# A four-layer hybrid kernel on one core: the first state-space steps are put in another order, and two of them move inside the branches of the feed-forward phase before

## The reference

```python
x = x + _L0_attn_a_ref(_layernorm(x), ...)   # a gated delta rule, in 256 steps of a recurrence
x = x + _L0_ffn_ref(_layernorm(x), ...)      # silu(x @ Wg.T) * (x @ Wu.T) @ Wd.T, hidden size 384
x = x + _L0_attn_b_ref(_layernorm(x), ...)   # a state-space layer (below)
x = x + _L0_ffn_ref(_layernorm(x), ...)      # the same feed-forward weights again
```

```python
zxbcdt = hidden_states @ W_in
z, xBC, dt = ...                                   # 256, 512 and 4 columns
xBC = jax.nn.silu(_causal_dwconv(xBC, conv_w, conv_b))   # 4 taps along the tokens
dt = jax.nn.softplus(dt + dt_bias)                 # the steps, one for each of 4 heads
A = -jnp.exp(A_log)
y = _ssd(x, dt, A, Bm, Cm) + x * D[None, None, :, None]  # sums over the past, decaying by exp(sums of dt * A)
y = y * jax.nn.silu(z)
y = y * jax.lax.rsqrt(jnp.mean(y * y, axis=-1, keepdims=True) + EPS) * norm_w
return y @ W_out
```

## Time and profile before

| | us |
|---|---|
| median of 3 runs | 880.91 (879.55 to 883.13) |
| the profiled execution | 879.69 |
| its span, first to last instruction | 877.9 |
| so around the span | 1.8 |
| PE busy | 773.3 (88%) |
| DVE busy | 621.8 (71%) |
| ACT busy | 535.7 (61%) |
| POOL busy | 561.6 (64%) |

### The profile page before, as it was taken

One profiled execution on the slowest core, in us unless ns is written; L12 is line 12 of the kernel. 1 busy time (PEld: TensorE's weight loads), 2 busy tenths in 40 slices (PEclk: granted clock), 3 DMA queues, 4 the chain that ended last, 5 costly groups with the idle time before them and its releaser, 6 DMA issues. The chain is left out here.

```text
span 877.9 us, 16088 instructions
## 1 busy us (share of the span) xinstructions
PE 773.3 (88%) x5146; PEld 551.7 (63%) x5146; DVE 621.8 (71%) x1739; ACT 535.7 (61%) x1035; POOL 561.6 (64%) x901
## 2 busy tenths in 40 slices
PE   1369999999999895999856999999999999959997
PEld 1258888888888774666634456656555555545665
DVE  1357878777878753888664678888887777637885
ACT  2224443443345323888644878978887788828986
POOL 1267567666766620788711579778868876757785
PEclk9979999999999999999955899999999999979999
DMA  7511111111111100000000000000000000000112
GB/s 195 134 28 37 46 28 28 38 46 28 28 42 41 29 14 1 1 1 0 2 0 8 1 1 3 7 1 2 9 0 1 7 4 1 1 0 25 48 49 73
DMA packets 59420, 22.16 MB, mean 25 GB/s; under 512 B 22224, under 2 KB 59088, under 8 KB 59344
## 3 DMA queue, kind: packets, MB, share of 16 engines
q1 hardware_dynamic: 59344, 21.23, 9.5%
HBM read 11.59 MB, written 9.63 MB: 24 GB/s over the span
## 5 line engine op out<-in xcount | busy, mean ns | idle before, releaser
L1405 DVE SCALAR_TENSOR_TENSOR arena<-bank,convw_sb,arena 128x510 f32<-128x510 f32 (+2 forms) x192 | 142.4, 744 | 42.2 <-ACT arena L898 37.5
L667 POOL TENSOR_TENSOR arena<-arena 128x768 f32<-128x768 f32 x64 | 114.9, 1815 | 12.8 <-ACT arena L925 10.9
L641 POOL TENSOR_TENSOR arena<-ff,arena 128x512 f16<-128x512 f32 x64 | 73.6, 1159 | 23.0 <-ACT arena L867 21.0
L571 POOL TENSOR_TENSOR leaf_tmp<-leafV 32x14 f32<-32x14 f32 (+6 forms) x224 | 55.8, 249 | 37.1 <-DMA leafV<-LT_dram 21.8
L862 ACT ACTIVATE ff<-bank 128x512 f32<-128x512 f32 x96 | 56.2, 586 | 32.2 <-PE bank L1708 32.0
L770 ACT ACTIVATE ff<-bank 128x256 f32<-128x256 f32 (+2 forms) x80 | 33.9, 424 | 65.1 <-PE bank L1549 37.7
L575 POOL TENSOR_TENSOR leafV<-leafV,leaf_tmp 32x14 f32<-32x14 f32 (+6 forms) x224 | 62.3, 278 | 17.6
L1795 PE MATMUL bank<-xnT,win_sb 128*128 128x512 f32 x128 | 71.8, 645 | 0.0
L1221 DVE SCALAR_TENSOR_TENSOR ff<-bank,ff 128x512 f32<-128x512 f32 x96 | 64.6, 684 | 8.9 <-ACT ff L862 8.0
L919 ACT ACTIVATE arena<-bank 128x384 f32<-128x384 f32 x128 | 59.8, 492 | 15.5 <-PE bank L1810 15.3
L755 ACT ACTIVATE xnT<-bank 128x512 f32<-128x512 f32 x34 | 20.3, 596 | 79.1 <-PE bank L1536 79.0
(11 more groups left out here) (199 smaller groups left out, 2239.2 us busy)
## 6 DMA issues: line engine op xcount, KB each, us to landing
LT_dram<-arena SPq DMA_DIRECT2D x16, 256.0 KB, 2.4
ff<-R_dram SPq DMA_DIRECT2D x16, 256.0 KB, 3.0
out<-x_all SPq DMA_DIRECT2D x8, 512.0 KB, 3.2
x_all<-in_L_attn_a_x SPq DMA_DIRECT2D x7, 512.0 KB, 7.3
ff<-pieces_dram SPq DMA_DIRECT2D x48, 6.0 KB
x_all<-in_L_attn_a_x SPq DMA_DIRECT2D x2, 256.0 KB, 3.6
R_dram<-tab SPq DMA_DIRECT2D x2, 256.0 KB, 2.7
leafV<-LT_dram SPq DMA_DIRECT2D x16, 32.0 KB, 2.7
```

What stands on the lines that cost most here:

```text
L571: nc.gpsimd.tensor_tensor(prod, V[:, s:s + 1, s + 1:LEAF].broadcast_to([leaf_rows, s, below]), V[:, 0:s, s:s + 1].broadcast_to([leaf_rows, ...
L641: nc.gpsimd.tensor_tensor(of_block(hl[u], j), hidT[u][:, j, :], of_block(hh[u], j), ALU.subtract).then_inc(hl_done[u], 1)
L667: nc.gpsimd.tensor_tensor(score[h], cb[g % 2], hgam[h], ALU.mult).then_inc(score_done, 1)
L1405: nc.vector.scalar_tensor_tensor(acc_of[:, :, s:SEQ], src_of[:, :, 0:SEQ - s], convw_sb[:, r, TAPS - 1 - s:TAPS - s], acc_of[:, :, s:SEQ], ...
```

## The change

The same work is done by the same instructions; only their order and place differ. (What goes into the branches stands in PE's list twice, and is run once.)

- DVE: the statistics of groups 2 and 3 go from the end of `ffn(0)` into the two halves of its last pair, behind `hidden(1)` and ahead of `add_residual`. `shift_ahead(2)` stands ahead of the last `add_residual`. `taps(0, 0)` goes from behind `with_bias(1)` to between `softplus_end(0)` and `chunk_sums(0)`; `taps(0, 1)` goes from ahead of `softplus_middle(0)` to behind `split_first`; `with_bias(4)` and `shift_ahead(6)` stand among the sums.
- ACT: the exponential of `A_log`, with its table load, goes to the head of the run-in, and `exp_of_quad(0)` goes ahead of both first taps.
- PE: `of_token(0)`, `transposes` of group 2 and `of_token(1)` go into the If and the Else branch, as `first_tokens`. Behind the branches the products of `dt` go ahead of the convolution's.
- POOL: the powers for groups 2 and 3 go ahead of `set_rows(0)`.

```diff
@@ POOL
+            ln_rstd_of(2 * GROUPS + 2, 2)
+            ln_rstd_of(2 * GROUPS + 3, 3)
             pool.wait_ge(x_done, done(2 * GROUPS - 2))
             set_rows(0)
-            for g in range(2, LN_LEAD + 1):
+            for g in range(4, LN_LEAD + 1):
@@ ACT
+            nc.scalar.activation(aexp_row[:, :], alog_row[:, :], ACT.Exp).then_inc(aexp_done, 1)
             normalise_ahead(2)
             normalise_ahead(3)
-            first_tap(0, 0)
             feature_major_ahead(2)
             feature_major_ahead(3)
             normalise_ahead(4)
+            normalise_ahead(5)
+            exp_of_quad(0)
+            first_tap(0, 0)
+            feature_major_ahead(4)
             first_tap(0, 1)
-            nc.scalar.activation(aexp_row[:, :], alog_row[:, :], ACT.Exp).then_inc(aexp_done, 1)
-            feature_major_ahead(4)
-            exp_of_quad(0)
-            normalise_ahead(5)
             feature_major_ahead(5)
+            normalise_ahead(6)
             first_tap(0, 2)
-            normalise_ahead(6)
             feature_major_ahead(6)
             normalise_ahead(7)
             feature_major_ahead(7)
+            normalise_ahead(8)
             first_tap(0, 3)
-            normalise_ahead(8)
@@ DVE, in ffn_half
                     if i + 2 <= PAIRS:
                         pair_stats(i + 2, u)
+                    else:
+                        ahead(u)
                     if prev is not None:
                         add_residual(1 - u, prev)
@@ DVE
-            ffn(0, weights_ready, first_stats)
+            ffn(0, weights_ready, lambda u: stats_ahead(2 + u), lambda: shift_ahead(2))
@@ DVE, the run-in
+            shift_ahead(3)
             with_bias(0)
-            shift_ahead(2)
-            shift_ahead(3)
             stats_ahead(4)
             with_bias(1)
-            taps(0, 0)
             stats_ahead(5)
+            shift_ahead(4)
             with_bias(2)
-            shift_ahead(4)
+            shift_ahead(5)
             with_bias(3)
             softplus_begin(0)
-            shift_ahead(5)
-            taps(0, 1)
             softplus_middle(0)
...
             softplus_end(0)
             stats_ahead(6)
+            taps(0, 0)
             chunk_sums(0)
             diffs_first()
+            shift_ahead(6)
+            with_bias(4)
             running_sums(0)
             split_first()
-            shift_ahead(6)
             stats_ahead(7)
+            with_bias(5)
+            shift_ahead(7)
+            taps(0, 1)
+            stats_ahead(8)
+            with_bias(6)
             taps(0, 2)
-            shift_ahead(7)
-            stats_ahead(8)
-            with_bias(4)
-            with_bias(5)
             shift_ahead(8)
+            with_bias(7)
             taps(0, 3)
-            with_bias(6)
-            with_bias(7)
             softplus_begin(1)
@@ PE
-            def ffn(run):
+            def ffn(run, after):
...
                 with pe.If(fits > 0):
                     ffn_of(run, True)
+                    after()
                 with pe.Else():
                     ffn_of(run, False)
+                    after()
...
+            def first_tokens():
+                pe.wait_ge(x_done, upto(2 * PAIRS, 0))
+                of_token(0)
+                turn_ahead(2)
+                of_token(1)
+
+            ffn(0, first_tokens)
@@ PE, the run-in
-            of_token(0)
-            of_token(1)
-            conv(0, 0)
-            turn_ahead(2)
             turn_ahead(3)
             of_token(2)
             of_token(3)
+            conv(0, 0)
+            turn_ahead(4)
             conv(0, 1)
-            turn_ahead(4)
-            turn_ahead(5)
             pe.wait_ge(z_done, done(QUAD - 1))
             steps_to_rows(0)
-            conv(0, 2)
-            turn_ahead(6)
+            turn_ahead(5)
             pe.wait_ge(chain_step, CSUM_AT)
             of_token(4)
+            conv(0, 2)
             of_token(5)
+            turn_ahead(6)
+            of_token(6)
+            turn_ahead(7)
             conv(0, 3)
-            turn_ahead(7)
-            of_token(6)
             of_token(7)
```

More of the change, by code:

```diff
@@ L1178, in _, with ffn @@
             in_order(attention_half, ahead)
-            def ffn(run, meanwhile, at_end):
+            def ffn(run, meanwhile, ahead, at_end):
                 phase = 2 * run + 1
@@ L1263, in shift_ahead @@
                 shift_at(2 * GROUPS + g, g)
-            def first_stats():
-                stats_ahead(2)
-                stats_ahead(3)
-            ffn(0, weights_ready, first_stats)
+            ffn(0, weights_ready, lambda u: stats_ahead(2 + u), lambda: shift_ahead(2))
             def add_residual(e):
@@ L1511, in _ @@
                 space_half(*ssd_half(h), [quad_at(h, stage) for stage in range(QUAD)])
-            ffn(1, lambda: None, lambda: None)
+            ffn(1, lambda: None, lambda u: None, lambda: None)
         @block.tensor
@@ L1768, in _ @@
             pe.wait_ge(later_in, 16 * LATER_DMAS)
-            ffn(0)
-            pe.wait_ge(x_done, upto(2 * PAIRS, 0))
             def of_token(d):
@@ L1781, in of_token, with turn_ahead @@
                 last.then_inc(dt_mm, 1)
+            def turn_ahead(g):
+                if g > 2:
+                    pe.wait_ge(xnT_done, done(2 * GROUPS + g - 1))
+                transposes_of(2 * GROUPS + g, g, mid_bank[0])
+            def first_tokens():
[4 more added lines that the diff above has]
+            ffn(0, first_tokens)
             def steps_to_rows(q):
@@ L1923, in space_half @@
                     conv(b, 3)
-            def turn_ahead(g):
-                if g > 2:
-                    pe.wait_ge(xnT_done, done(2 * GROUPS + g - 1))
-                transposes_of(2 * GROUPS + g, g, mid_bank[0])
-            of_token(0)
-            of_token(1)
-            conv(0, 0)
-            turn_ahead(2)
             turn_ahead(3)
@@ L1957, in _ @@
                 space_half(*ssd_half(h), quad_at(h, 2))
-            ffn(1)
+            ffn(1, lambda: None)
 _INS = ['L0_attn_a_x', 'L0_attn_a_Wq', 'L0_attn_a_bq', 'L0_attn_a_Wk', 'L0_attn_a_bk', 'L0_attn_a_Wv', 'L0_attn_a_bv',
```

## The result

The changed kernel takes 872.27 us (median of 4 runs, 870.45 to 874.25), the kernel before beside it 880.62 us; the ratio is 0.9906, with a 95% interval of 0.9877 to 0.9936. In a second series of 12 runs it was 0.9922 (0.9895 to 0.9949). The profiled execution took 871.66 us, its span is 869.9 us, 8.0 less than 877.9.

The account below looks back on a forecast made before the run. PE bounds the steady phases, a chain of waits between engines the run-in; the terms led to 7.9 to 8.6 us of lead, taken as -8.0 from the profiled 879.69, so 871.7, or 872.9 as median; range 868.5 to 877.5.

Parts of the forecast that it names:

- the smaller lead: Start of the loop: ACT's activations lead by 7.9 us, token_major(0, 1) by 8.6; the smaller was to count.
- Statistics in the halves: Last feed-forward pair: statistics ahead of each residual delay PE once, 0.35 us, taken as +0.3; bounds 0 and 0.7.
- First products inside the branches: PE, start of the run-in: the 2.21 us issue gap moves behind of_token(1) and stays; bounds 0 and 4.4.
- Covered, by half a microsecond: Normalisation of group 2 on ACT: done at 434.2 us, before PE wants it at 434.7.
- Up to the fourth bias: Step products and biases behind the gap: fourth bias ends at 444.2 us against 447.15, lead 2.9.
- rival B: Better PE clock behind the run-in as well, with the gap gone too: 869.4 us, chance 0.15.
- The exponential: ACT, ahead of the softplus denominator: taken at once, denominator at 444.8 against 451.93 us; greatest gain, 4.2.
- Taps ahead of the sums: DVE: with taps(0, 0) between, the sums start at 452.2 against 456.98 us, so the lead falls to 4.8.
- The rest of DVE's list: DVE up to softplus_begin(1): second dt_nabs at 471.9 against 478.78 us, lead 6.9, with new waits of 1.3 and 2.0.
- The end: Second dt_nabs to token_major(0, 1): 474.9 against 483.52 us, lead 8.6, as the two gates no longer hold it.
- Rival C: Part is given back through a low clock in the loop's first halves or a 4.4 us gap: 876.9 us, chance 0.20.
- rivals D and E: D: loop's start held elsewhere, order does nothing, 880 us, chance 0.06; E: PE stays at 1.2 GHz, 886 us, chance 0.04.

Follow-up runs that it names:

- e9: The changed kernel as it is, profiled a second time: 873.49 us, ratio 0.9922.
- e12: The kernel before as it is, profiled a second time: 882.1 us, one run.
- e2: Changed kernel with the statistics of groups 2 and 3 back at the end of the first feed-forward phase, ahead of the last residual: 876.35 us, ratio 0.9951.
- e4: Changed kernel without the Else branches and the choice between them on PE: 870.40 us, ratio 0.9894.
- e1: Changed kernel with the first step products and the transposes of group 2 behind the two branches again: 874.09 us, ratio 0.9922.
- e5: Changed kernel with seven more PE steps inside the branches, up to the transposes of group 5: 872.77 us, ratio 0.9921.
- e3: Changed kernel with ACT's exponential and table load behind both first taps, and both taps ahead of the softplus on DVE: 875.31 us, ratio 0.9932.
- e6: Changed kernel with taps(0, 0) behind split_first instead of ahead of chunk_sums(0): 870.93 us, ratio 0.9889.
- e11: Changed kernel with shift_ahead(6) and with_bias(4) behind split_first on DVE instead of among the sums: 872.2 us, one run.
- e7: Kernel before with only A_log's exponential at the run-in's head, exp_of_quad(0) ahead of first_tap(0, 1), taps(0, 1) behind split_first: 879.08 us, ratio 0.9996.
- e10: Changed kernel with PE's steps up to group 5's transposes inside the branches, plus 38 useless products in four idle places: 875.98 us, ratio 0.9948.

## Why the prediction was right, step by step

The forecast was 872.9 us, the time is 872.3; the span fell by exactly the 8.0 us of the sum. That exactness is luck. Two terms were off by about 1 us each and in opposite directions, and in the second pair of profiles (e9 and e12) the lead is 8.5 us at `token_major` and 6.2 at the second feed-forward phase. The two series of runs give ratios of 0.9906 and 0.9922, 8.3 and 6.9 us of 881. A gain of this kind and about this size is shown, not one of 8.0. (The sum says 8.0 where "the smaller lead" was 7.9.)

- *Statistics in the halves*, +0.3: 5.27 - 4.91 = 0.36. Right. e2 shows what they buy: without them `token_major` is 1.3 to 1.5 us later.
- *First products inside the branches*: the gap was moved, not removed, with 2.33 us. That it goes with the branches is shown by e4, and that it goes with the place of the jump by e1 and e5. The move itself buys nothing (e1: 1.1 us less without it). I had not priced the move alone, only its steps in the chain; "Covered, by half a microsecond" was wrong for the normalisation of group 2, and a sign of being wrong that I had named was there: PE waited 0.45 us. The step product ahead of it ran in 0.95 us, and the table load, "not dearer where it is now", did hold the normalisation up by some 0.5 us, as e3 shows.
- *Up to the fourth bias*, lead 2.9: `dt_nabs` was 3.8 us earlier by the times of the two profiles. The mis-sized term is the length of the steps ahead of the jump, 4.34 us in the sum and 2.85 in the trace, since the step products took 0.95 us and not 1.64. The better clock at this place stood in rival B, not in the sum. But the 1.64 itself belonged to one execution: in e12 the kernel before did its first step product in 1.02 us, and of the lead at `dt_nabs`, 4.1 us in the first pair, 2.2 are left in the second.
- *The exponential*, 4.2: from `dt_nabs` to the denominator 4.75 before and 0.54 after, so 4.21. Right as a stage. As the "greatest gain of the change" it must be read with e3: undone with the taps coming in its place it costs 1.6 to 1.8 us at `token_major`. In e3 2.2 us come back at the first sums, ahead of which `taps(0, 0)` is already done, and another 1.9 up to the second `dt_nabs`, with `taps(0, 1)` no longer in that part of the list.
- *Taps ahead of the sums*, -2.3: denominator to first sums 5.05 before, 7.26 after, 2.2 us. Right; and e6 shows in its trace that it is no loss.
- *The rest of DVE's list*, lead growing by 2.1: first sums to second `dt_nabs` 21.80 before, 19.49 after, 2.3. The waits that I foresaw of 1.3 and 2.0 us were 1.34 and 0.39 + 1.81. Which of the moves on PE and ACT brings it is open; by e11 it isn't the place of `shift_ahead(6)` and `with_bias(4)`.
- *The end*, 1.7: second `dt_nabs` to `token_major` 4.74 before, 3.08 after. Right.
- *"The smaller lead counts"*: I let 0.6 of 8.6 go to the loop. It took 1.7 of 9.8 in the first pair of profiles: 18.25 us to `head_outputs` instead of 16.55. The changed kernel's window 480 to 488 shows the cause that goes with it, granted 0.50 with PE busy throughout. Over 14 profiles this stretch took 13.4 to 18.3 us; where the clock was 1.00 in its full part (e3, e12) it took 14.0 and 13.4. In the second pair 2.9 of 8.5 us went (16.32 instead of 13.41). How much of it belongs to the changed order and how much to chance is open, as the two profiles of the changed kernel, 18.25 and 16.32, and the two of the kernel before, 16.55 and 13.41, overlap. Rival C had the mechanism, with about 4 us as its price; and its sign, a lower clock than before in the first halves, was there in the first profile.
- The rivals D and E are out: what lead there was at `head_outputs` was kept through the loop, 8.1 us and 8.0 at the end in the first profiles, 5.6 and 6.2 in the second pair.

Taken back one at a time, the parts that have an experiment are worth 1.3 to 1.5 us (e2), 1.6 to 1.8 (e3), 0.7 to 1.0 (e6), nothing (e11) and less than nothing (e1) at `token_major`, together some 4 us of 8.5 to 10.0. No experiment takes back the rest alone: on PE the products of `dt` ahead of the convolution's, on POOL the powers ahead of `set_rows(0)`, on ACT and DVE the remaining order. That these bring the rest is argued from the starts in the trace, not shown. A sign of their size is e1, which has them all, with the statistics in the halves, and starts its run-in with the gap, as e12 does: its `dt_nabs` comes at 17.42 instead of 20.97.

No version here is shown to beat the changed kernel. e5 gains 1.9 to 2.1 us of run-in in its trace, and its runs, 0.9921 (0.9897 to 0.9944), show no difference.

## What to carry to other kernels

Between two full phases, write the run-in down as a list of starts, engine by engine, from the rows, and look for an engine that holds a short, early result behind long work; here a 0.25 us exponential stood behind a table load and a tap, and its result came 4 us late until it was moved. At `token_major` that was worth 1.6 to 3.8 us (e3, e7), and alone, in e7, nothing in the runs. A stage that gets shorter isn't yet a gain: what was moved out of the way comes back in the list of the same engine, so only the time at which the next phase starts counts. And where executions differ more than the change, compare traces from a common event close ahead of it, and profile the same program twice before a difference of 2 us is explained.

## What was not expected of the hardware

The jump over the Else code has no fixed price: TensorE's gap there was 2.21 and 1.87 us in two profiles of the kernel before, 2.33 and 2.61 in two of the changed kernel, 1.95 in e1 and 2.87 in e2, and 4.17 in e10, where it stood eight groups of work further on. At that same place a wait of 3.11 us hid it whole in e5. The first phase of the same program ended 5.7 us apart in two executions. And TensorE's granted clock stood at 0.50, which is the 1.2 GHz level, over 8 us in which PE was busy all the time, and at 1.00, the 2.4 GHz level, over as full a stretch of e12. Ahead of the low stretch PE had waited 1.90 us for ACT, then 0.56 and 1.11 us; in e12 it had waited 1.12 us for ACT at the place of the last of these, and the clock stayed at 1.00. In e10 PE was not idle at all from 474.30 us on, behind a wait of 2.96 us for ACT, and the clock was 0.50 from 476 to 488.
